# New step orders for all five engines in a two-layer graph attention kernel, and banks for transposed probabilities by count

## What is computed

```python
def layer0(h, adj):                       # B=32, T=256, H=384, 6 heads of 64
    q, k, v = heads(h @ Wq + bq), heads(h @ Wk + bk), heads(h @ Wv + bv)
    scores = einsum('bhqd,bhkd->bhqk', q, k) / 8
    probs = softmax(scores + where(adj, 0.0, NEG)[:, None], axis=-1)
    return merge(einsum('bhqk,bhkd->bhqd', probs, v)) @ Wf + bf

def layer1(h, adj):                       # 12 heads of 32
    hh = einsum('bnd,ade->bane', h, W)
    src, dst = tanh(hh) @ w_src, tanh(hh) @ w_dst
    attn = leaky_relu(src + swapaxes(dst, 2, 3), 0.2)
    attn = softmax(where(adj, attn, -999.0), axis=-1)
    out = elu(merge(einsum('banm,bame->bane', attn, hh) + b))
    gate = sigmoid(h @ H_w.T + H_b)
    return gate * out + (1 - gate) * h

h = maximum(layernorm(x), 0);  x = x + layer0(h, adj)
h = maximum(layernorm(x), 0);  x = x + layer1(h, adj)
```

## Time and profile before

| | us |
|---|---|
| median of 3 runs | 1311.48 |
| lowest, highest | 1309.01, 1311.65 |
| span of the profiled execution | 1309.3 |
| PE, ACT, DVE, POOL busy in it | 1265.7, 1251.5, 1209.1, 913.2 |
| one pass of the loop (38.95 us): PE, ACT, DVE, POOL busy | 38.95, 38.52, 36.99, 28.2 |

### The profile page before, as it was taken

The page is one execution under the profiler, slowest core; times in us unless marked ns, Lnnn a source line. Parts: engine busy times, 40 slices in busy tenths (PEclk is TensorE's granted clock), DMA queues, the critical chain, the costliest instruction groups (busy, mean ns, idle before and its releaser), DMA issues.

```text
span 1309.3 us, 33375 instructions
## 1 busy us (share of the span) xinstructions
PE 1265.7 (97%) x10511; PEld 918.9 (70%) x10511; DVE 1209.1 (92%) x4401; ACT 1251.5 (96%) x3701; POOL 913.2 (70%) x1106
## 2 busy tenths in 40 slices
...
ACT  5699999999999999999999999999999999999986
...
DMA packets 29854, 33.74 MB, mean 26 GB/s; under 512 B 10481, under 2 KB 29681, under 8 KB 29681
## 3 DMA queue, kind: packets, MB, share of 16 engines
...
## 4 chain that ended last, share of the span: by engine, by line
PE 88%; ACT 3%; DVE 3%; POOL 2%; DMA 1%; issue 1%; SPq 1%; POOLq 0%; DVEq 0%; ACTq 0%
PE job L623 27%; PE pt L696 18%; PE job L635 14%; PE unit L670 7%; PE job L718 7%; PE job L764 6%; PE job L611 4%; PE unit L687 3%; PE job L773 2%; ACT p L874 1%; DMA xb<-in_x_dram 1%; PE job L619 1%; POOL prod L1282 1%; ACT pT L884 1%; DVE y L1051 1%
## 5 line engine op out<-in xcount | busy, mean ns | idle before, releaser
L874 ACT ACTIVATE p<-y,min 128x256 f32<-128x256 f32 x768 | 394.1, 539 | 0.9 <-DVE min L1125 0.8
L1119 DVE SCALAR_TENSOR_TENSOR unit<-unit,s,dst 128x256 f32<-128x256 f32 x768 | 335.8, 482 | 14.0 <-issue 1.7
L696 PE MATMUL pt<-ident,p 128*128 128x128 f32 x2304 | 331.5, 275 | 12.3 <-ACT p L874 7.1
L623 PE MATMUL job<-w,h 128*128 128x384 f16 x1728 | 311.1, 326 | 1.8 <-DVE h L1024 1.7
L696 PEld LDWEIGHTS pt<-ident,p 128*128 128x128 f32 x2304 | 268.3, 142 | 42.9 <-ACT p L874 14.0
L1125 DVE CUSTOM_DVE_ANT_0 y<-unit,mask 128x256 f32<-128x256 f32 x768 | 290.5, 414 | 0.0
L1260 POOL TENSOR_SCALAR p<-p,rec 128x256 f32<-128x256 f32 x384 | 178.7, 481 | 123.3 <-DVE rec L1058 122.9
L623 PEld LDWEIGHTS job<-w,h 128*128 128x128 f16 x1728 | 168.6, 98 | 97.3 <-DVE h L1024 2.5
L884 ACT ACTIVATE pT<-pt 128x512 f32<-128x512 f32 x384 | 232.3, 624 | 1.6 <-PE pt L696 1.6
L635 PE MATMUL job<-h,w 128*128 128x256 f16 x1728 | 216.4, 274 | 2.3 <-DVE h L1024 2.1
L830 ACT ACTIVATE p<-y,min 128x256 f32<-128x256 f32 x384 | 191.0, 503 | 13.8 <-PE pt L696 7.9
...
## 6 DMA issues: line engine op xcount, KB each, us to landing
...
```

Of the source, the lines that this page charges most:

```text
L623: last = mm(bank[:, 0:H], rows[:, i, c, t * P:(t + 1) * P], w16[:, w, j, c, :], start=n == 0, stop=(c, i, j) == (NC - 1, *TERMS[-1]))
L696: last = nc.tensor.transpose(pt_ps[u % 2][:, (2 * hh + kt) * P:(2 * hh + kt + 1) * P], probs[:, u % 3, hh, kt * P:(kt + 1) * P], ident[:])
L874: last = op(p1[:, u % 3, hh, :], y1[:, u % YB, hh, :], ACT.Exp, bias=min1[:, u, hh:hh + 1], scale=-1.0, accum_out=sum1[:, t, h:h + 1])
L1119: V.scalar_tensor_tensor(leaky[:, hh * T:(hh + 1) * T], bank[:, hh * T:(hh + 1) * T], s8[par][:, t, h:h + 1], dst5[:, c % 2, hh, :], ALU.a ...
```

## The change

All tables are new: `STARTING`, `ORDERS` and `ENDING` of all five engines hold the same steps in other orders. SyncE's list now has its own bounds (its start covers two passes, not three), so that a load of x stands ahead of the load of an earlier batch's adjacency. The two banks of the transposed probabilities are given out by the running count of PT0 and PT1 units on TensorE (`prob_bank`), with one semaphore for each bank, so that units of both layers may follow one another in any parity; PV0 and PV1 wait for the last two units' banks. EXP0 and EXP1 wait for the transposes of the unit that used the same buffer, three before, of their own layer alone. A few waits that the old order implied are written out: for LOAD_ADJ on MASK0, for STATS0 and AGGREGATE1 on RSTD, for RSTD on NORM, for SKIP on OUT_SUM.

The diff, without the tables' rows:

```diff
-LAG = {"L": -2, "P": -1, "A": 0, "B": 1, "C": 2, "D": 3}
+LAG = {"J": -4, "K": -3, "L": -2, "P": -1, "A": 0, "B": 1, "C": 2, "D": 3, "E": 4}
...
 ORDERS = {
     "PE": steps("""
-        B PV1 0, P QK 0, L LN_T0 0, B PT1 9, B PT1 10, P QK 1, A GATE 1, B PT1 11, P QK 2, L LN_T0 1, P PT0 0,
+        L LN_T0 0, B PV1 0, P QK 0, B PT1 9, B PT1 10, P QK 1, A GATE 1, P PT0 0, L LN_T0 1, B PT1 11, P QK
...
     "SP": steps("""
-        L LOAD_X 0, C STORE 0, L LOAD_ADJ 0
+        L LOAD_X 0, P LOAD_ADJ 0, C STORE 0
...
-FIRST, LAST = 3, 2
+FIRST = {"PE": 3, "ACT": 3, "DVE": 3, "POOL": 3, "SP": 2}
+LAST = {"PE": 2, "ACT": 2, "DVE": 2, "POOL": 2, "SP": 2}
 
 
 def sequence(engine, n_batch):
 
     order = list(STARTING[engine])
-    for n in range(FIRST, n_batch - LAST):
+    for n in range(FIRST[engine], n_batch - LAST[engine]):
...
-        s_pT = sem("s_pT_in_sbuf")
+        s_pT = [sem(f"s_pT_in_sbuf{i}") for i in range(2)]
...
+        def prob_bank(b, step, u):
+
+            n = n_t.before(b, step, u)
+            return pt_ps[n % 2], s_pT[n % 2], n // 2
...
-                    used = n_mask1.after(b.back(2), "MASK1")
-                    sp.wait_ge(s_mask1, used)
+                    sp.wait_ge(s_mask0, n_mask0.after(b.back(2), "MASK0"))
+                    sp.wait_ge(s_mask1, n_mask1.after(b.back(2), "MASK1"))
...
-                last = {n_job.bank(b, step, idx): (step, idx) for step, idx in needs}
-                for bank, (step, idx) in last.items():
+                last = {}
+                for step, idx in needs:
+                    bank = n_job.bank(b, step, idx)
+                    last[bank] = max(last.get(bank, 0), n_job.after(b, step, idx))
+                for bank, value in last.items():
                     if bank != but:
-                        pe.wait_ge(s_done[bank], n_job.after(b, step, idx))
+                        pe.wait_ge(s_done[bank], value)
...
             def transpose_probs(b, step, u, probs):
-                if n_t.some_before(b, step, u, 1):
-                    pe.wait_ge(s_pT, n_t.before(b, step, u, 1))
+                bank, evacuated, used = prob_bank(b, step, u)
+                if used:
+                    pe.wait_ge(evacuated, used)
                 for hh in range(2):
                     for kt in range(NT):
-                        last = nc.tensor.transpose(pt_ps[u % 2][:, (2 * hh + kt) * P:(2 * hh + kt + 1) * P],
+                        last = nc.tensor.transpose(bank[:, (2 * hh + kt) * P:(2 * hh + kt + 1) * P],
                                                    probs[:, u % 3, hh, kt * P:(kt + 1) * P], ident[:])
                 last.then_inc(s_t, 1)
+
+            def wait_evacuated(b, step, u):
+
+                for unit in (u - 1, u):
+                    _, evacuated, used = prob_bank(b, step, unit)
+                    pe.wait_ge(evacuated, used + 1)
...
-                pe.wait_ge(s_pT, n_t.after(b, "PT0", (3, 5)[i]))
+                wait_evacuated(b, "PT0", (3, 5)[i])
...
             def exp0(b, par, u):
                 act.wait_ge(s_y0, n_y0.after(b, "SCORES0", u))
-                if n_t.some_before(b, "PT0", u, 2):
-                    act.wait_ge(s_t, n_t.before(b, "PT0", u, 2))
+                if u >= 3:
+                    act.wait_ge(s_t, n_t.after(b, "PT0", u - 3))
+                elif b.ref >= 1:
+                    act.wait_ge(s_t, n_t.after(b.back(1), "PT0", u + 3))
...
-                if n_t.some_before(b, "PT1", u, 2):
-                    act.wait_ge(s_t, n_t.before(b, "PT1", u, 2))
+                if u >= 3:
+                    act.wait_ge(s_t, n_t.after(b, "PT1", u - 3))
+                elif b.ref >= 1:
+                    act.wait_ge(s_t, n_t.after(b.back(1), "PT1", u + 9))
...
             def stats0(b, par, _):
                 dve.wait_ge(s_x[par], loaded(b))
+                if b.ref >= 1:
+                    dve.wait_ge(s_rstd, n_rstd.after(b.back(1), "RSTD0"))
...
             def aggregate1(b, par, _):
+                if b.ref >= 1:
+                    dve.wait_ge(s_rstd, n_rstd.after(b.back(1), "RSTD1"))
...
-            def make_rstd(k, step, sstep):
+            def make_rstd(k, step, sstep, s_used, n_used, user):
                 def part(b, par, _):
 
                     here = n_mv.after(b, sstep)
                     pool.wait_ge(s_mv, here)
+                    if b.ref >= 1:
+                        pool.wait_ge(s_used, n_used.after(b.back(1), user))
...
+                if b.ref >= 2:
+                    pool.wait_ge(s_sum, n_sum.after(b.back(2), "OUT_SUM"))
```

More of the change, by code:

```diff
@@ L80 @@
[L80 to L89, removed]
@@ L100 @@
[L100 to L109, removed]
@@ new lines @@
+        LOW_W 4 0, K 2 1, SKIP_H 0 0, SCORES0 2 1, LN_T1 0 0, LN_T1 1 0, SCORES0 3 1, NORMP0 2 1, SCORES0 4
+        1, LOW_W 5 0, GATE_BIAS 2 0, STATS0 0 3, LN_T0 0 2, LN_T0 1 2, NORMP0 3 1, NORMP0 4 1, SCORES0 5 1,
+        SCORE_SUM 0 0, NORMP0 5 1, DST_T 0 0, SCORES1 0 0, SCORES1 1 0, K 0 2, SCORES1 2 0, PV0 0 1, PV0 1
+        1, SCORES1 3 0, K 1 2, SCORES1 4 0, OUT0 0 1, OUT0 1 1, STATS1 0 1, STATS1 1 1, AGGREGATE1 0 1,
+        SCORES1 5 0, SCORES1 6 0, SCORES1 7 0, LN_T1 0 1, LN_T1 1 1, SCORES1 8 0, K 2 2, SCORES1 9 0,
```

230 lines of the change are left out of this document (123 added, 107 removed).

## The result

The changed kernel takes 1369.46 us (median of 4 runs, 1363.87 to 1374.15), the kernel before 1310.84 us beside it. The ratio is 1.0445, 95% interval 1.0417 to 1.0473: slower, where 1304 (1298 to 1311) had been forecast. The profiled execution is the slowest of the four (1374.15 us) and has a span of 1372.2 us.

The account below looks back on a forecast made before the run. TensorE was taken to bound the loop, with ScalarE 0.4 us behind. From 1309.3 us, the loop's -4.6 and the start's -1.5 gave 1303.2; with 0.8 added the forecast was 1304 us, range 1298 to 1311.

Parts of the forecast that it names:

- What bounds the kernel: Loop pass of 38.95 us: TensorE bounds it without a gap, ScalarE 0.4 us behind, VectorE busy 36.99.
- the first hand-over: Second scores need VectorE's first masked scores: 2.16 us after the first scores, against TensorE's 2.09, late by 0.07.
- TensorE's neighbours, -0.15 + 0.04: TensorE's loop order: fewer switches between transposes and L764 save 0.14 to 0.15 us; transposes after L718 cost 0.04.
- the strict reading of the rule: Scores straight into L764 on TensorE: the whole 0.14 us is paid again, leaving -0.8 us for the loop.
- Four hidden waits, -0.21: Small waits inside TensorE's matmul bars at L687 and the groups after it: -0.21 us a pass if all go.
- Hand-overs, +0.15: Waits between engines in the loop's new orders: give back 0.15 us of a pass, 0.04 to 0.43.
- the slower rival: ScalarE's unbroken run makes PV1 1 late on TensorE; at 0.45 us a pass the kernel takes 1316; chance 0.13.
- forecast pass of 38.78: One pass of the loop in the new orders, from 38.95 us with a net -0.17.
- First steps, -1.5: Start of the kernel: earlier loads of x for batches 1 and 4 save 1.5 us (-4 to +2).
- Last steps, 0: Tail of the kernel: its last links stay in order, so 0 us (-1.5 to +2).
- Waits written out, banks by count: zero: Bank semaphores by count and written-out waits on all engines: they ask for steps already done, cost zero.
- Sum: Whole kernel: profiled run 1309.3 less 4.6 for the loop and 1.5 for the start, 0.8 added, predicts 1304 us.

Follow-up runs that it names:

- e1: Changed kernel with both FINISH steps right after SCORES1 8 in VectorE's loop order, no longer after SCORES1 11: 1311.01 us, ratio 0.9997.
- e2: Changed kernel with GpSimd's SCORE_PROD cut to fewer columns from batch 3 on (scores wrong), all orders kept: 1304.34 us, ratio 0.9945.
- e3: Kernel before with both FINISH steps moved after SCORES1 11, beside SCORE_PROD, in VectorE's loop order: 1405.64 us, ratio 1.0717.
- e5: Changed kernel with both FINISH steps right behind K 2 in VectorE's loop order, ahead of SCORES1 9: 1307.36 us, ratio 0.9968.
- e10: e5 with GpSimd's SKIP moved behind GATES, ahead of RSTD1 and NORM1: 1305.85 us, ratio 0.9953.
- e8: e5 with the first steps of TensorE, ScalarE, VectorE and GpSimd as in the kernel before, new loads kept: 1314.05 us, ratio 1.0021.
- e12: Kernel before with HIGH_W 0 moved behind SUM_W 3 among ScalarE's first steps: 1312.74 us, ratio 1.0009.
- e6: e5 with the last steps of TensorE, ScalarE, VectorE and GpSimd as in the kernel before: 1307.48 us.
- e4: Changed kernel's code with all step orders and loop bounds of the kernel before: 1311.28 us, ratio 0.9999.

## Why the prediction was wrong, by its own steps

- **What bounds the kernel.** TensorE, with ScalarE 0.4 us behind: right, and too narrow. VectorE's 36.99 of 38.95 were read as room, and the part on the loop speaks of a change in VectorE's order only at SCORE_SUM. That both FINISH steps move right in front of the masked scores that TensorE waits for isn't in the sum. This is the step that failed: the first hand-over ("late by 0.07") was taken from rows in which FINISH stands elsewhere, and the moved FINISH steps were put at nothing. The runs show 2.5 us of standing on VectorE and a QK 1 that is 2.2 us late in each pass, with the clock's loss on top; e1 and e2 take it away, e3 brings it into the kernel before. At its old length FINISH would have been costed too low as well, since that length holds only beside the old neighbours on GpSimd.
- **It could be seen before.** The kernel before has one FINISH beside SCORE_PROD, behind its loop. VectorE there:

```profile
1230.70 1.19 DVE L1169 SCALAR_TENSOR_TENSOR y<-o1m,gate 128x768 f32<-128x768 f32 x1
```

It starts during GpSimd's second product, which ends at 1231.06, and ends 0.8 behind that; the third piece then takes 2.43. GpSimd there, and beside FINISH 0 in the middle of the loop (the 0.81 is 0.19 elsewhere):

```profile
597.90 0.81 POOL L1222 TENSOR_SCALAR nmean<-mv 128x2 f32<-128x2 f32 x1 [1.67 <-DVE mv L995]
...
1231.14 2.43 POOL L1288 TENSOR_TENSOR prod<-prod 128x768 f32<-128x768 f32 x1
```

- **TensorE's neighbours, -0.15 + 0.04.** Right. L779 follows L678 by 1.06 (633.71 to 634.77) as any group does, so the strict reading of the rule in the Trainium skill's "TensorEngine Tiling (Array Packing)", section "Key Properties", with the drain paid once more at this border, does not hold here. TensorE's busy time in a pass is 38.81.
- **Four hidden waits, -0.21.** Two of them went; with QK 1 on time (e5) the nine f16 matmuls still take 1.07 instead of 0.98 and the four behind them 0.47 instead of 0.44.
- **Hand-overs, +0.15.** The first is the one that broke: 2.16 forecast, 4.39 measured. With the lock away it is 2.20 (e1, e2, e5, e10), late by 0.1 against TensorE's 2.09. PV1 1, on which the slower rival rested, stands 1.06 behind QK 2 in the changed kernel and in e5, without a wait. The rival's sign was right, its place and size (1316) were wrong. The forecast pass of 38.78 is measured at 38.83 (e10) and 38.85 (e2, e5): 0.1 x 27 = about 3 us of gain, not 4.6.
- **First steps, -1.5.** The sign was right, the size and the reason wrong. The changed kernel is 6.4 us ahead at QK 0 of batch 4 (172.59 instead of 178.98), and 5.0 at batch 5, one slow pass later. Both waits for x named there are gone: VectorE reads x of batch 1 at 12.32 (21.06 in the earlier trace rows), and x of batch 4 goes out at 84.42 (100.26) and is read at 90.91 without idle time. But the new loads alone, with the old first steps of the other engines, give nothing (e8). The 4.5 us wait of HIGH_W had been passed over; e12 shows that its removal gives 0.09 us at QK 0 and nothing in the time. Which orders of batches 0 to 3 carry the gain stays open.
- **Last steps, 0.** Right as to the orders (e6). Of the 5.4 us of the changed kernel 2.2 are the last pass's wait. The rest isn't shown to be theirs: with the same last steps the stretch takes anything from 117.2 (e10) to 122.1 us (e8).
- **Waits written out, banks by count: zero.** Right (e4).
- **Sum.** Without most of the lock the change gives -4 us (e5) and, GpSimd's SKIP moved too, -6 (e10, 1305.85). That e2, with SCORE_PROD cut, comes to 1304.3, the forecast's number, is in part luck: the loop gives about 3 us instead of 4.6, and the start 5.7 instead of 1.5. The sum also began with the span, 1309.3, as the execution's own time; wherever a run lists both, its time is 1.8 to 2.1 us above its span, so the 0.8 that was added is about 1 us short. Beside 58 us that is nothing.
